# A second stopping place for GpSimd within each chunk's gathers, in the second sweep of a two-layer graph network

## The chip, the cores and the metric

The kernel runs on one core of one Trainium2 chip. The metric is the device time of one execution in microseconds; lower is better. The engines of the core are TensorE (PE, matmuls; PEld, its weight loads), VectorE (DVE), ScalarE (ACT), GpSimd (POOL) and SyncE (SP), which each work off a queue of their own and wait for one another through semaphores. GpSimd issues the indirect gathers here, SyncE nearly all the other transfers.

## The reference

Two layers over a graph of 12500 nodes with 128 features and 200000 edges (src, dst), the edges sorted by dst. A preceding layer norm and a relu stand before each layer, and each result is added to x.

```python
# layer 1
neigh = segment_sum(h[src], dst);  x = x + relu(relu(((1 + eps) * h + neigh) @ W1 + b1) @ W2 + b2)
# layer 2, on h = layernorm(relu(layernorm(x)))
t = gelu(concat([h[src], edge_vector], 1) @ Wt + bt)         # per edge
attn = sum((t @ Wk + bk) * (h[dst] @ Wq + bq), -1) * edge_type / sqrt(128)
e = exp(attn - segment_max(attn, dst)[dst]);  a = e / segment_sum(e, dst)[dst]
aggr = segment_sum(a * (t @ Wv + bv), dst);   x = x + (residual + gelu(aggr))
```

## The kernel before, in words

The 200000 edges are cut into 98 chunks of 2048 edges (CHUNK); a chunk is 16 columns of 128 edges, and four columns are a quad. The first sweep (`gin_sweeps`) does layer 1 and writes, for each node, its row of h @ Wt to DRAM (`source_rows`, `arow` in the code) and the vectors for the scores. The second sweep (`attention_sweeps`) does layer 2. It keeps running maxima and sums in windows of nodes, so that one pass over the chunks is enough.

In the second sweep, chunk c passes through stages; in step n each engine works on chunk n in the stage `f`, on n-1 as `mid`, on n-2 as `late`, on n-3 as `last` and on n-4 as `e`. The order within a step is written out by hand in the function `step` of each engine. The last four places of the pipeline matter less here; what counts is:

- GpSimd (lines 1115 to 1127) gathers the 16 columns of chunk c from `source_rows` into one of four buffers `t`, one indirect DMA per column (`gather_chunk`, issued in line 514), with a semaphore for each quad. It waits first for the chunk's list of sources, then for `t_used`, which counts the sums of chunk c-4 (the buffer's last reader), and then makes a `hold`: a multiplication of one element (line 508) that waits for the preceding hold's own count and so stands in GpSimd's queue as an instruction.
- TensorE, step n: turns quad 0 of chunk n into `pre_ps` and adds the edge features' product (lines 1140 and 1144), adds up the totals of n-3, turns quad 1, turns the gelu of quad 0 back (line 1153) and makes its score products (line 1167, semaphore `sc_q`, one count per quad), turns the scores of n-1, turns quad 2, then the gelu and the scores of quad 1, the block maxima of n-1 (line 1183), the end products of n-4, quads 3, 2 and 3 in the same manner, spreads the running maxima (line 1189), clears the sum banks and makes the sums of n-2 (line 1210, `t_used`, four counts per chunk).
- ScalarE makes the gelu of each quad (line 1281) and copies the turned result over the gathered rows in `t` (line 1285).
- VectorE adds the bias to the scores (line 1359), picks each edge's score, raises the window's maxima (line 1419) and keeps the accumulators.
- SP loads the list of sources, the edge features in two halves (line 1073), weights and windows. It loads the list of chunk c when the last quad of chunk c-2 has landed.

The first four steps and the last ones are written out, those between are a loop over four chunks each.

Of the kernel before, what the change touches and what calls it, by code (L numbers as in the profile page):

```python
# [43 lines left out]
QUADS = COLS // 4  # L44
# [31 lines left out]
def wait(eng, sem, value):  # L76

    if isinstance(value, int) and value <= 0:
        return
    eng.wait_ge(sem, value)  # L80
# [36 lines left out]
def over_chunks(eng, step):  # L117


    step(Chunk(None, 0), None)  # L120
    for n in range(1, PEEL):
        step(Chunk(None, n), Chunk(None, n - 1))
    with engine_loop(eng, 0, (NCH - PEEL - 2) // 4) as i:
        for n in range(PEEL, PEEL + 4):
            step(Chunk(i, n), Chunk(i, n - 1))
    for n in range(NCH - 2, NCH):
        step(Chunk(None, n), Chunk(None, n - 1))
    step(None, Chunk(None, NCH - 1))
# [375 lines left out]
def hold(gp, g, held, c):  # L504


    wait(gp, held, c)
    gp.tensor_tensor(g["spare"][0:1, 0:1], g["ones"][0:1, 0:1], g["ones"][0:1, 0:1], ALU.mult).then_inc(held, 1)  # L508


def gather_chunk(gp, idx, rows, out, done, op=ALU.bypass, cols=range(COLS)):

    for k in cols:
        gp.indirect_dma_start(out=out[:, k, :], out_offset=None, in_=rows[:, :], compute_op=op,  # L514
                              in_offset=bass.IndirectOffsetOnAxis(ap=idx[:, k:k + 1], axis=0)).then_inc(done, 16)
# [452 lines left out]
def attention_sweeps(nc, a, g, arow, qk, ck, fades, first, res, span):  # L968
# [4 lines left out]
    with ExitStack() as ctx:  # L973
# [37 lines left out]
        held = st.sem("held")  # L1011
# [9 lines left out]
        s = {k: st.sem("a_" + k) for k in names}  # L1021
# [34 lines left out]
        with nc.Fori(0, span + 1, WIN):  # L1056
            with nc.Block() as block:
# [57 lines left out]
                @block.gpsimd  # L1115
                def _(gp):
                    def step(f, bk):
                        if f:
                            if f.at == 3:
                                gp.wait_ge(w["tables"], 7)  # L1120
                            wait(gp, idx_in[f.j], 16 * (f.h + f.j))
                            wait(gp, s["t_used"], PARTS * (f.c - 3))
                            hold(gp, g, held, f.c)
                            for q in range(QUADS - 1 if f.last else QUADS):
                                gather_chunk(gp, g["idx0"] if f.at == 0 else idx[f.j], arow, t[f.k], gathered[f.k][q],
                                             cols=range(4 * q, 4 * q + 4))
                    over_chunks(gp, step)
# [395 lines left out]
```

## Time and profile before

| | us |
|---|---|
| median of 3 runs | 4087.96 (4086.41 to 4090.1) |
| span of the profiled execution | 6013.6 |
| POOL busy in it | 3043.9 |
| PE busy | 3985.3 |
| DVE busy | 1961.7 |
| ACT busy | 1601.6 |

The profiled execution is much longer than the timed ones. Its rows tell what each instruction took and what it waited for in that execution. An engine's idle time has a releaser: the work whose semaphore ended the wait; "issue" is idle time for which none is seen, and "remote" one whose source the profile doesn't tell. A time in a row of the timeline is the start since the beginning of the span.

### The profile page before, as it was taken

The page shows a single profiled execution, that of the slowest core. Times are in us where ns is not written, and L with a number is a line of the kernel's source. Part 1 is how long each engine was busy: PE and PEld are TensorE (multiplying, and loading weights), DVE is VectorE, ACT ScalarE, POOL GpSimd, SP SyncE. Part 2 cuts the span into 40 slices and gives each one's busy share as a digit, 9 for nine tenths or more (in the row PEclk, how much of TensorE's full clock was granted, in tenths as well). Part 3 has the DMA queues.
Part 4 walks back from the last instruction along what each step waited for, and adds up shares of the span by engine and source line. Part 5 has one row for each costly group of instructions (what it writes and reads, how often), then busy time and mean ns, then how long its engine had stood idle before and what let it go on. Part 6 is the DMA issues. An engine that isn't in the chain of part 4 may idle for free.

```text
span 6013.6 us, 75137 instructions
## 1 busy us (share of the span) xinstructions
PE 3985.3 (66%) x19120; PEld 3071.2 (51%) x19121; DVE 1961.7 (33%) x6898; ACT 1601.6 (27%) x3223; POOL 3043.9 (51%) x3332
## 2 busy tenths in 40 slices
PE   1466666555555555577777777777777777777777
PEld 1344444444434444355555555556555565555655
DVE  4222222222222222233333333333333333333344
ACT  4222222222222222322222222222222222222223
POOL 4566666666666666344444444444444444444442
PEclk5555555555565555577766667766676666766677
DMA  4122222222222222222222222222222222222222
GB/s 128 53 68 66 65 67 66 65 67 67 66 65 68 66 65 67 62 81 77 81 77 77 82 76 80 78 78 81 75 81 77 76 82 76 81 77 77 82 77 65
DMA packets 390065, 446.29 MB, mean 74 GB/s; under 512 B 111768, under 2 KB 314734, under 8 KB 390000
## 3 DMA queue, kind: packets, MB, share of 16 engines
q1 hardware_dynamic: 276940, 233.83, 13.3%
q0 software_dynamic: 100096, 205.20, 13.1%
q10 hardware_dynamic: 12964, 6.53, 0.4%
q8 instruction: 25, 0.41, 0.0%
q14 instruction: 40, 0.33, 0.0%
HBM read 387.05 MB, written 58.21 MB: 74 GB/s over the span
## 4 chain that ended last, share of the span: by engine, by line
another core or an unknown queue 28%; PE 25%; ACT 3%; issue 2%; DVE 0%; DVEq 0%; ACTq 0%
PE attention_sum_ps L1210 10%; PE attention_t_ps L1153 4%; PE attention_pre_ps L1144 3%; PE attention_sc_q L1167 3%; PE attention_row_bank L1189 2%; PE attention_pre_ps L1140 2%; ACT attention_tT L1281 2%; ACT attention_t L1285 1%; PE attention_tot_ps L1219 1%; PE attention_tot_ps L1202 1%; PE attention_sum_ps L1201 0%; DVE attention_lines L1419 0%; ACT acc L1043 0%; PE attention_xm_bank L1175 0%
## 5 line engine op out<-in xcount | busy, mean ns | idle before, releaser
L514 POOL DMA_INDIRECT attention_t<-source_rows,attention_idx x1548 | 1471.4, 951 | 496.0 <-issue 496.0
L514 POOL DMA_INDIRECT gin_hs<-h_rows,gin_idx x1500 | 1455.8, 971 | 486.1 <-issue 486.1
L508 POOL TENSOR_TENSOR spare<-ones 1x1 f32<-1x1 f32 x195 | 36.0, 184 | 1892.9 <-PE attention_sum_ps L1210 1376.9
L1281 ACT ACTIVATE attention_tT<-attention_pre_ps 128x512 f32<-128x512 f32 x391 | 233.5, 597 | 1883.5 <-remote 1381.9
L1167 PE MATMUL attention_sc_q<-attention_qw,attention_tT 128*128 x3128 | 590.7, 329 | 187.7 <-issue 187.6
L1167 PEld LDWEIGHTS attention_sc_q<-attention_qw,attention_tT 128*128 128x128 f32 x3128 | 540.7, 247 | 215.6 <-issue 215.4
L698 PE MATMUL gin_sums<-gin_hot,gin_hs 128*128 128x40 f32 x3136 | 612.2, 383 | 0.0
L1210 PE MATMUL attention_sum_ps<-attention_e_hot,attention_t 128*128 128x96 f32 x3072 | 607.5, 389 | 0.0
L698 PEld LDWEIGHTS gin_sums<-gin_hot,gin_hs 128*128 128x128 f32 x3136 | 598.1, 297 | 18.2 <-issue 12.6
L1210 PEld LDWEIGHTS attention_sum_ps<-attention_e_hot,attention_t 128*128 128x128 f32 x3072 | 591.8, 301 | 21.4 <-issue 20.9
L706 PE MATMUL gin_uy_bank<-acc,gin_w_W 128*128 x196 | 118.6, 708 | 727.2 <-DVE acc L926 727.1
L1419 DVE TENSOR_TENSOR attention_lines<-attention_lines,attention_row_bank 1x40 f32 x784 | 144.3, 184 | 1235.3 <-remote 1139.5
L1153 PE MATMUL attention_t_ps<-ident,attention_tT 128*128 128x128 f32 x1564 | 315.3, 338 | 340.4 <-ACT attention_t L1285 256.8
L1153 PEld LDWEIGHTS attention_t_ps<-ident,attention_tT 128*128 128x128 f32 x1564 | 229.1, 172 | 602.2 <-issue 314.8
L1144 PE MATMUL attention_pre_ps<-attention_evT,attention_w_edge 128*128 128x512 f32 x782 | 475.6, 695 | 0.0
L706 PEld LDWEIGHTS gin_uy_bank<-acc,gin_w_W 128*128 128x128 f32 x196 | 49.2, 312 | 763.9 <-issue 763.9
L1140 PE MATMUL attention_pre_ps<-ident,attention_t 128*128 128x128 f32 x1564 | 284.1, 311 | 208.5 <-issue 150.5
L926 DVE TENSOR_TENSOR acc<-acc,gin_sums 128x264 f32 x98 | 42.1, 430 | 1032.9 <-remote 1017.6
L1140 PEld LDWEIGHTS attention_pre_ps<-ident,attention_t 128*128 128x128 f32 x1564 | 199.5, 160 | 245.1 <-issue 179.8
L1285 ACT ACTIVATE attention_t<-attention_t_ps 128x512 f32<-128x512 f32 x391 | 232.9, 596 | 338.3 <-remote 253.5
L804 ACT ACTIVATE gin_n_zT<-gin_c_bank,eps 128x256 f32<-128x256 f32 x98 | 46.5, 474 | 980.1 <-remote 955.3
L1434 DVE TENSOR_TENSOR attention_masked<-attention_masked,attention_row_bank 128x80 f32<-128x80 f32 x784 | 126.6, 232 | 211.1 <-PE attention_row_bank L1189 210.8
(215 smaller groups left out, 5319.1 us busy)
## 6 DMA issues: line engine op xcount, KB each, us to landing
attention_evT<-in_edge_attr_cols SPq DMA_DIRECT2D x196, 512.0 KB
attention_t<-source_rows,attention_idx POOLq DMA_INDIRECT x1548
gin_hs<-h_rows,gin_idx POOLq DMA_INDIRECT x1500
attention_qw<-qk_cols SPq DMA_DIRECT2D x98, 160.0 KB, 3.2
attention_cw<-qk_bias_cols SPq DMA_DIRECT2D x98, 132.0 KB, 3.9
attention_fade<-fades SPq DMA_DIRECT2D x98, 132.0 KB, 3.8
gin_x<-in_x SPq DMA_DIRECT2D x98, 128.0 KB
residual_rows<-gin_r SPq DMA_DIRECT2D x98, 128.0 KB
```

Of the source, the lines that this page charges most:

```text
L514: gp.indirect_dma_start(out=out[:, k, :], out_offset=None, in_=rows[:, :], compute_op=op, in_offset=bass.IndirectOffsetOnAxis(ap=idx[:, k: ...
L698: mm = pe.matmul(sums[j][:, bass.ds(off, WIN)], hs[bk.k][:, k, :], hot[j][:, k, :], start=False, stop=True, skip_group_check=True)
L706: pe.matmul(u_ps, W["W1"][:, :], g["acc"][:, bass.ds(at, MW)], start=True, stop=False)
L1140: pe.matmul(pre_ps[:, k * P:(k + 1) * P], t[f.k][:, 4 * q + k, :], g["ident"][:, :], is_transpose=True, start=(k == 0), stop=False, skip_g ...
L1144: pe.matmul(pre_ps[:, :], w_edge[:, :], evT[q // 2][:, 512 * (q % 2):512 * (q % 2 + 1)], start=False, stop=True, skip_group_check=True).th ...
L1153: mm = pe.transpose(t_ps[:, k * P:(k + 1) * P], tT[q % 2][:, k * P:(k + 1) * P], g["ident"][:, :])
L1167: mm = pe.matmul(sc_ps[:, o:o + WIDE], tT[q % 2][:, (n % 4) * P:(n % 4 + 1) * P], qw[j][:, bass.ds(off, WIDE)], start=True, stop=True)
L1210: mm = pe.matmul(sum_of(bk)[:, bass.ds(off, WIDE)], t[bk.k][:, k, :], e_hot[j][:, k, :], start=False, stop=True, skip_group_check=True)
L1281: act.activation(tT[q % 2][:, :], pre_ps[:, :], ACT.Gelu).then_inc(s["tT_sb"], 1)
L1285: act.activation(t[f.k][:, 4 * q:4 * q + 4, :].rearrange("p k d -> p (k d)"), t_ps[:, :], ACT.Copy).then_inc(s["t_sb"], 1)
L1419: v.tensor_tensor(some, some, row_bank[0:1, b * WIN:(b + 1) * WIN], ALU.max).then_inc(s["raised"], 1)
L1434: v.tensor_tensor(masked[j][:, cols, :], masked[j][:, cols, :], row_bank[:, bass.ds(off, WIN)].unsqueeze(1).to_broadcast([P, SUB, WIN]), A ...
```

## The change

At half of a chunk's quads GpSimd waits until `sc_q` has reached 4(c-1) + 2, that is, until the score products of quads 0 and 1 of chunk c-1 are done, and makes a second hold. The hold's counter therefore goes up by two per chunk. The first sweep is as it was.

```diff
                             wait(gp, s["t_used"], PARTS * (f.c - 3))
-                            hold(gp, g, held, f.c)
+                            hold(gp, g, held, 2 * f.c)
                             for q in range(QUADS - 1 if f.last else QUADS):
+                                if q == QUADS // 2:
+                                    wait(gp, s["sc_q"], QUADS * (f.c - 1) + QUADS // 2)
+                                    hold(gp, g, held, 2 * f.c + 1)
                                 gather_chunk(gp, g["idx0"] if f.at == 0 else idx[f.j], arow, t[f.k], gathered[f.k][q],
                                              cols=range(4 * q, 4 * q + 4))
```

QUADS is 4 and PARTS is 4. For chunk 0 the value is negative and `wait` leaves the wait out.

## Rows read from the trace of the kernel before

**Rows 1.** The page: span, busy time, and the granted clock in 40 slices.
```profile
span 6013.6 us, 75137 instructions
...
PE 3985.3 (66%) x19120; PEld 3071.2 (51%) x19121; DVE 1961.7 (33%) x6898; ACT 1601.6 (27%) x3223; POOL 3043.9 (51%) x3332
...
PEclk5555555555565555577766667766676666766677
```

**Rows 2.** Groups on GpSimd, second sweep: busy us, mean ns, idle before, releasers.
```profile
L514 POOL DMA_INDIRECT attention_t<-source_rows,attention_idx x1548 | 1471.4, 951 | 496.0 <-issue 496.0
L508 POOL TENSOR_TENSOR spare<-ones 1x1 f32<-1x1 f32 x97 | 17.9, 184 | 1457.4 <-PE attention_sum_ps L1210 1376.9 <-issue 55.6 <-DMA attention_idx<-in_src_chunks 24.9
L514 POOL DMA_INDIRECT attention_t<-source_rows,idx x16 | 15.6, 975 | 5.1 <-issue 5.1
```

**Rows 3.** The same groups in the first sweep.
```profile
L514 POOL DMA_INDIRECT gin_hs<-h_rows,gin_idx x1500 | 1455.8, 971 | 486.1 <-issue 486.1
L514 POOL DMA_INDIRECT gin_hs<-in_x,gin_idx x44 | 42.7, 970 | 13.3 <-issue 13.3
L508 POOL TENSOR_TENSOR spare<-ones 1x1 f32<-1x1 f32 x97 | 17.9, 184 | 366.1 <-remote 257.0 <-DMA h_rows<-gin_hg 64.0 <-issue 29.2
```

**Rows 4.** Timeline, GpSimd, between the sweeps: start us, us, instruction, idle before.
```profile
2411.36 0.94 POOL L514 DMA_INDIRECT gin_hs<-h_rows,gin_idx  x1 [0.30 <-issue]
2481.72 0.18 POOL L508 TENSOR_TENSOR spare<-ones 1x1 f32<-1x1 f32 x1 [69.42 <-POOLq L234]
...
2501.65 0.94 POOL L514 DMA_INDIRECT attention_t<-source_rows,idx  x1 [0.30 <-issue]
2502.61 0.18 POOL L508 TENSOR_TENSOR spare<-ones 1x1 f32<-1x1 f32 x1
2502.94 0.98 POOL L514 DMA_INDIRECT attention_t<-source_rows,attention_idx  x1 [0.15 <-issue]
```

**Rows 5.** Timeline of a steady chunk: GpSimd, and one quad of TensorE.
```profile
4499.83 0.18 POOL L508 TENSOR_TENSOR spare<-ones 1x1 f32<-1x1 f32 x1 [15.57 <-PE attention_sum_ps L1210]
...
4500.49 0.98 POOL L514 DMA_INDIRECT attention_t<-source_rows,attention_idx  x1 [0.48 <-issue]
...
4504.74 0.60 PE L1140 MATMUL attention_pre_ps<-ident,attention_t 128*128 128x128 f32 x4
...
4506.48 1.03 PE L1167 MATMUL attention_sc_q<-attention_qw,attention_tT 128*128 x8
...
4509.28 0.95 POOL L514 DMA_INDIRECT attention_t<-source_rows,attention_idx  x1 [0.30 <-issue]
...
4519.29 0.95 POOL L514 DMA_INDIRECT attention_t<-source_rows,attention_idx  x1 [0.30 <-issue]
...
4535.04 0.18 POOL L508 TENSOR_TENSOR spare<-ones 1x1 f32<-1x1 f32 x1 [14.81 <-PE attention_sum_ps L1210]
...
4535.71 0.98 POOL L514 DMA_INDIRECT attention_t<-source_rows,attention_idx  x1 [0.48 <-issue]
```

**Rows 6.** Timeline of the same chunk: ScalarE and VectorE, released by TensorE.
```profile
4520.97 0.60 ACT L1285 ACTIVATE attention_t<-attention_t_ps 128x512 f32<-128x512 f32 x1 [4.30 <-remote]
...
4523.35 2.39 DVE L1419 TENSOR_TENSOR attention_lines<-attention_lines,attention_row_bank 1x40 f32 x8 [11.89 <-remote]
```

**Rows 7.** Timeline, TensorE: the sums and the first half of the next step.
```profile
4529.03 5.85 PE L1210 MATMUL attention_sum_ps<-attention_e_hot,attention_t 128*128 128x96 f32 x32
...
4534.72 0.60 PE L1140 MATMUL attention_pre_ps<-ident,attention_t 128*128 128x128 f32 x4
...
4541.69 0.47 PE L1167 MATMUL attention_sc_q<-attention_qw,attention_tT 128*128 x3
```

**Rows 8.** Timeline, GpSimd: the last gather of the execution.
```profile
5944.36 0.94 POOL L514 DMA_INDIRECT attention_t<-source_rows,attention_idx  x1 [0.30 <-issue]
```

**Rows 9.** All holds: duration in ns, shortest, median, longest.
```profile
L508 POOL TENSOR_TENSOR spare<-ones x195: 184/184/188, 34.0 to 5929.9; 1x1 f32<-1x1 f32 x195
```

**Rows 10.** Groups between 4000 and 5000 us: two of VectorE's with two SBUF inputs.
```profile
L1389 DVE TENSOR_TENSOR acc<-acc,attention_fade 128x264 f32 x28 | 12.0, 428 | 2.9 <-issue 2.9
...
L1422 DVE TENSOR_TENSOR attention_mdiff<-rows,attention_lines 1x264 f32<-1x264 f32 x28 | 11.8, 422 | 1.0
```

## The prediction

> **What bounds the kernel now.** I read the head of the page first, because its span and the time to be predicted differ: the profiled execution spans 6013.6 us [rows 1], the median of the unprofiled runs is 4088.0 us, with a spread of 4 us. The recorded execution is 1.47 times as long as the ones that are timed. So no row may be taken over as a share of the time; what is to be asked of each row is whether it can still be true when 1925 us are gone. No time of the profiled execution other than its span is given, so the sum below is made in steps of the span and carried to the median by a budget.
>
> The second view is GpSimd alone, once for each sweep. In the second sweep it issued 1548 + 16 indirect gathers of 951 ns and 975 ns with 496.0 + 5.1 us of idle time between them that nothing released ("issue", some 0.3 us each), and 97 one-element multiplications (the holds) of 17.9 us in all: 1471.4 + 15.6 + 496.0 + 5.1 + 17.9 = 2006.0 us of work. Beside it stand 1457.4 us of idle time ahead of the holds, nearly all released by the sums on TensorE [rows 2]. In the first sweep the same sum is 1455.8 + 42.7 + 486.1 + 13.3 + 17.9 = 2015.8 us, with 366.1 us of waiting [rows 3]. Both sweeps need 4022 us of GpSimd, and some 60 us less if no hold has to be woken (below). The whole unprofiled execution takes 4088. The 1457 + 366 us of waiting at the holds must therefore be almost entirely an effect of the recorded execution: in the timed runs GpSimd works from end to end. What is left is 66 to about 126 us. The start takes 34.0 of them up to the first hold [rows 9], and the gap between the sweeps (2412.3 to 2481.7, 69.4 us here [rows 4]) and the end after the last gather (5945.3 to 6013.6, 68.3 us here [rows 1, 8]) want more than the remaining 32 to 92 us already.
>
> The third view is TensorE in a steady chunk. Its first half, from the turning of quad 0 to the scores of quad 1, goes from 4534.72 to 4541.69 + 1.03 = 4542.7 us at the full clock: 8.0 us [rows 7], the last 1.03 being what eight score products take at 4506.48 [rows 5]. The rest I estimate from rows of the same clock: two quads of 4504.74 to 4507.51 = 2.8 us [rows 5] less some 1.3 us for the turning of quad 2, which is counted already, the sums with 5.85 us [rows 7], and 2.5 to 3.7 us, a guess, for spreading the maxima, the end products and the clearing. That gives about 20.6 to 21.8 us per chunk as recorded, against 2006.0 / 98 = 20.5 us for GpSimd. The two engines are level in the second sweep, within what these rows can tell; the budget above says that TensorE can't be much over 20.7 us either. I take it that the bound of the second sweep is GpSimd or a tie, and that the granted clock is near full there: the trace has 6 and 7 tenths [rows 1], but with TensorE waiting a large part of its step.
>
> **The change, part by part.** Three things change, all on GpSimd's queue in the second sweep.
>
> First, the hold at a chunk's start waits for the count 2c instead of c. It is the hold's own counter and it is already there. No cost.
>
> Second, each of the 98 chunks gets a second hold after its second quad of gathers. What a hold costs when nothing keeps it waiting is seen at the second chunk: the last gather of chunk 0 starts at 2501.65, the hold at 2502.61, the first gather of chunk 1 at 2502.94 [rows 4]. From gather to gather that is 1.29 us. Without a hold it is (4509.28 - 4500.49) / 7 = 1.256 us [rows 5]. So an unhindered hold costs 0.04 us, since it slips into the 0.3 us between gathers: 98 x 0.04 = 4 us if GpSimd sets the end, 0 if TensorE does. When it does have to wait, waking costs more: from the hold's start to the next gather 4535.71 - 4535.04 = 0.67 us [rows 5] against 0.33 us unhindered, so 0.38 us in all beyond the wait, or 98 x 0.38 = 37 us. No unhindered hold stands inside the loop in this trace, where the wait's value is also computed in registers; for that the 0.38 us is the upper end too. I take 0.04, since that row is the same instruction in the same place of the queue, already satisfied.
>
> Third, the wait itself. Behind it on GpSimd's queue are the eight gathers of quads 2 and 3 of chunk c, then everything of chunk c+1; the list loads are SP's and are not queued behind it, but SP waits for the last quad of a chunk before it overwrites its list, so it inherits a delay. It is released by the score products of quad 1 of chunk c-1. The earliest start of chunk c's gathers is the end of the sums of chunk c-4, which is the start of TensorE's step c-1. The eight gathers and the hold then need 4509.28 + 0.95 - 4499.83 = 10.4 us [rows 5]; TensorE needs 8.0 us from the start of that step [rows 7]. So even where GpSimd is as far ahead as it may be, the release comes 2.4 us before it is asked for, and where GpSimd is behind (it is the bound) it comes earlier still. Wait: 0.
>
> A cover that is gone must be priced too. Suppose the release comes x us into the step, later than 10.4. Quads 2 and 3 then end at x + 0.7 + 10.0, so the next chunk starts x + 10.7 - P into the next step of length P, and its own first half ends 10.4 us after that, which is past x whenever 21.1 > P. The wait does not add up from chunk to chunk: it moves idle time from the chunk's start to its middle. TensorE feels it only if quad 3 is late for its turning, about 9 us into step c: for P = 20.6 with some 2 us for a landing, x would have to exceed 16 us.
>
> A hold could also be held up by VectorE, if the two meet at SBUF. A step has five VectorE instructions with two SBUF inputs (fades and maxima), 0.42 us each [rows 10], 2.1 us of 20.6; a tenth of the new holds would meet one and wait some 0.2 us: 98 x 0.1 x 0.2 = 2 us more. Against it, all 195 holds of the trace lie between 184 and 188 ns [rows 9], though VectorE was busy for a third of the span [rows 1]. This is rival (d). The Trainium skill, in "SBUF — State Buffer", section "Who interferes with whom", has the rule behind it: a VectorE instruction with two SBUF inputs contends with a GpSimd instruction that reads SBUF, and the later one blocks. The trace does not bear it out for the holds.
>
> Sum: 4088 + 4 us if GpSimd bounds the second sweep, 4088 + 0 if TensorE does. I forecast 4091 us.
>
> **The rivals.** (a) The wait bites, and the time ends above. The recorded execution speaks for it. There TensorE's completions reach the others late: ScalarE copies quad 1 only at 4520.97 us, and VectorE starts raising the maxima, released by a product queued right behind the scores of quad 1, at 4523.35 us [rows 6]. The step began at about 4499.8, so x is between 21 and 23.5 us of 35.2. The same share of a step of 20.6 us would be 12 to 14 us, past 10.4. Then GpSimd wakes at each middle, 0.38 us, and where it is the bound that is 98 x 0.38 = 37 us: 4125 us. It decides from the point at which the scores of quad 1 come more than 10.4 us after the gathers' start while GpSimd has no idle time elsewhere. Against it: a wait delays the next chunk, and from then on the release is earlier than the demand, so not every chunk would pay. A milder form, 0.1 to 0.2 us per hold for the registers in the loop, gives 4098 to 4108 us. Chance 0.25 for both.
>
> (b) The pause helps TensorE. In the trace its completions stay away just while gathers are issued (4500.5 to 4520.2) and come in a rush afterwards [rows 5, 6]. If a rest of that exists without the recording, a pause at a chunk's middle lets them through. Against it: GpSimd is busy for nearly the whole timed execution, so a pause that is really taken costs what it gives. The most that can be won is what GpSimd idles in the second sweep; of the 32 to 92 us left in the budget, which the gap and the end want as well, I let a third of the upper figure lie there: 4088 - 30 = 4058 us. Chance 0.18.
>
> (c) The change does nothing to time because the second sweep is bound by TensorE, whose steps GpSimd's holds cannot reach: 4088 us. This and the +4 us of the forecast can't be told apart here; both are "no change". Together 0.52.
>
> (d) VectorE's two-input instructions hold up some of the new holds. With one in ten late by 0.2 us it is 4088 + 4 + 2 = 4094 us. The even durations of all holds [rows 9] speak against it. Chance 0.05.
>
> **How the numbers follow.** About 0.2%, 8 us, is what a measurement of this kernel tells from no change. Forecast, (c) and (d), 4088 to 4096: 0.52 + 0.05 = 0.57, same. Rival (a), 4098 to 4125: 0.25, slower. Rival (b), 4058 to 4079: 0.18, faster. The range takes in both ends of the hold's cost and both rivals' prices: 4058 to 4126 us.
>
> **What the changed profile would show.** The holds would be 293 instead of 195, with 184 ns each. In the second sweep a middle hold would follow the eighth gather. In the recorded execution, where completions are late, I expect it to wait: from about 10.4 to some 23 us into the chunk, 11 to 13 us each. The last eight gathers then end near 33.9 us, just before the release of the next chunk at 35.2 us [rows 5], so the idle time ahead of the first hold shrinks from about 15 to 1 to 3 us and the span stays near 6010 us. If the span of the second sweep falls instead, completions were held back by the gathers, and (b) gains. If it grows by more than 1%, the wait bites and (a) gains. The prediction is wrong in its root if an unhindered hold in the loop is seen to cost more than 0.1 us from gather to gather, or if the gathers themselves are faster without the recording, so that GpSimd isn't the bound at all and TensorE's waits decide.

## The result and the profile after

| | us |
|---|---|
| before, median of 20 runs | 4088.1 (4080.8 to 4094.4) |
| after, median of 20 runs | 4095.7 (4086.8 to 4106.9) |
| ratio | 1.002, 95% interval 1.0013 to 1.0027 |
| forecast | 4091, range 4058 to 4126 |
| span of the profiled execution, before / after | 6013.6 / 4085.1 |

The change costs 7.6 us, 0.2%. The forecast said +3 and named no measurable change as the likeliest; the time lies in the range and just within the border, 4096 us, of what it called the same. The range is 68 us wide, so that the time fell into it says little; the terms are what is to be compared.

The profiled execution of the changed kernel is as long as the timed ones. Its page:

```profile
span 4085.1 us, 75424 instructions
...
PE 3302.9 (81%) x19120; PEld 2576.1 (63%) x19121; DVE 1932.0 (47%) x6898; ACT 1590.1 (39%) x3223; POOL 3046.0 (75%) x3430
...
PEclk6555555565655565555679999999999999999999
```

So much shorter a recording looks like a large gain of the change. It is none: the kernel before, recorded again, has a span of 4094.3 us (below). The 6013.6 us of [rows 1] belonged to that one recording. What produced it stays open; no run here tries it.

GpSimd in the second sweep, first after the change, then in the new recording of the kernel before; columns as in [rows 2], which they answer:

```profile
L514 POOL DMA_INDIRECT attention_t<-source_rows,attention_idx x1548 | 1481.2, 957 | 442.2 <-issue 428.1 <-PE attention_sc_q L1170 5.3 <-DMA attention_idx<-in_src_chunks 4.6
L508 POOL TENSOR_TENSOR spare<-ones 1x1 f32<-1x1 f32 x196 | 36.6, 187 | 31.4 <-POOLq L234 28.1
L514 POOL DMA_INDIRECT attention_t<-source_rows,idx x16 | 15.8, 990 | 4.9 <-issue 4.8 <-POOL spare L508 0.2
```

```profile
L514 POOL DMA_INDIRECT attention_t<-source_rows,attention_idx x1548 | 1479.6, 956 | 456.9 <-issue 452.5 <-DMA attention_idx<-in_src_chunks 4.0
L508 POOL TENSOR_TENSOR spare<-ones 1x1 f32<-1x1 f32 x98 | 18.4, 188 | 34.3 <-POOLq L234 32.5
L514 POOL DMA_INDIRECT attention_t<-source_rows,idx x16 | 15.6, 974 | 5.1 <-issue 5.1
```

The 1457.4 us of waiting ahead of the holds [rows 2] are gone in both: what is left is the gap between the sweeps, at the first hold. Without that gap, GpSimd works through the second sweep in 1481.2 + 442.2 + 36.6 + 15.8 + 4.9 = 1980.7 us after and 1479.6 + 456.9 + 18.4 + 15.6 + 5.1 = 1975.6 us before. Nor does any of the 98 new holds wait; the 5.3 us put down to `attention_sc_q` are 19 ordinary gaps of 0.3 us ahead of gathers. The groups leave out idle times as short as the 0.02 us ahead of a hold, so the length of the sweep tells more. From the start of its first gather to the end of its last one it took 1983.3 us after and 1976.7 us before: 6.6 us more, 0.07 us per new hold.

That the new recording of the kernel before is nevertheless the longer of the two, by 9.2 us, comes mostly from the first sweep, whose code is the same. From its first hold to its last gather it took 2001.1 us before and 1989.5 us after. One recording of each kernel can't show a change of 0.2%; why the first sweep varies is found below.

The timeline around a chunk's start (the hold at 3007.37) and its middle (3017.63) after the change, start and duration in us:

```profile
3005.74 1.03 PE L1170 MATMUL attention_sc_q<-attention_qw,attention_tT 128*128 x8
...
3006.41 0.94 POOL L514 DMA_INDIRECT attention_t<-source_rows,attention_idx  x1 [0.30 <-issue]
...
3007.37 0.18 POOL L508 TENSOR_TENSOR spare<-ones 1x1 f32<-1x1 f32 x1
...
3007.71 0.98 POOL L514 DMA_INDIRECT attention_t<-source_rows,attention_idx  x1 [0.15 <-issue]
...
3008.99 0.94 POOL L514 DMA_INDIRECT attention_t<-source_rows,attention_idx  x1 [0.30 <-issue]
...
3009.09 0.65 PE L1143 MATMUL attention_pre_ps<-ident,attention_t 128*128 128x128 f32 x4 [0.54 <-DMA attention_t<-source_rows,attention_idx]
...
3014.28 3.81 PE L1213 MATMUL attention_sum_ps<-attention_e_hot,attention_t 128*128 128x96 f32 x32
...
3017.63 0.18 POOL L508 TENSOR_TENSOR spare<-ones 1x1 f32<-1x1 f32 x1
```

Two things are to be read in it. TensorE waits for GpSimd, at quad 3 (3009.09), whose last gather has just landed; it follows GpSimd and not the other way round. It made the scores of quad 1 by 3006.8 us; the middle hold of the next chunk asks for them at 3017.6, 10.9 us later. And the price of a hold is complete only at the second gather behind it: from 3006.41 to 3008.99 are 2.58 us for two gathers, where two without a hold take 2.50. The hold fits into the idle 0.30 us all but some 0.05, and the gather behind it takes 0.98 us instead of 0.94.

### The profile page after: what moved, and what is told of

It reads as the page before. It is cut to its first block and busy times, and to the rows that moved or that the text cites. A ratio compares the mean times of both kernels' runs of the same rounds, so it can differ in the third digit from the quotient of the medians.

```text
span 4085.1 us, 75424 instructions
## 1 busy us (share of the span) xinstructions
PE 3302.9 (81%) x19120; PEld 2576.1 (63%) x19121; DVE 1932.0 (47%) x6898; ACT 1590.1 (39%) x3223; POOL 3046.0 (75%) x3430
## 5 line engine op out<-in xcount | busy, mean ns | idle before, releaser
L514 POOL DMA_INDIRECT attention_t<-source_rows,attention_idx x1548 | 1481.2, 957 | 442.2 <-issue 428.1
L514 POOL DMA_INDIRECT gin_hs<-h_rows,gin_idx x1500 | 1428.1, 952 | 443.8 <-issue 443.4
L698 PE MATMUL gin_sums<-gin_hot,gin_hs 128*128 128x40 f32 x3136 | 683.1, 412 | 0.0
L698 PEld LDWEIGHTS gin_sums<-gin_hot,gin_hs 128*128 128x128 f32 x3136 | 668.7, 328 | 22.3 <-issue 21.6
L1147 PE MATMUL attention_pre_ps<-attention_evT,attention_w_edge 128*128 128x512 f32 x782 | 420.6, 621 | 1.7 <-issue 1.7
L1170 PE MATMUL attention_sc_q<-attention_qw,attention_tT 128*128 x3128 | 409.8, 275 | 0.0
L1170 PEld LDWEIGHTS attention_sc_q<-attention_qw,attention_tT 128*128 128x128 f32 x3128 | 388.4, 195 | 0.0
L692 PE MATMUL gin_sums<-gin_zeros 1*128 1x264 bf16 x98 | 36.2, 369 | 412.5 <-DMA gin_hs<-h_rows,gin_idx 264.0
L1213 PE MATMUL attention_sum_ps<-attention_e_hot,attention_t 128*128 128x96 f32 x3072 | 365.9, 277 | 0.0
L1213 PEld LDWEIGHTS attention_sum_ps<-attention_e_hot,attention_t 128*128 128x128 f32 x3072 | 350.2, 192 | 11.9
L1156 PE MATMUL attention_t_ps<-ident,attention_tT 128*128 128x128 f32 x1564 | 245.6, 281 | 0.0
L492 ACT ACTIVATE gin_m_std<-gin_m_mv,ln_eps 128x2 f32<-128x2 f32 x294 | 85.2, 290 | 340.0 <-DVE gin_m_mv L486 339.5
```

The costliest lines, as they stand in the source:

```text
L492: act.activation(m["std"][:, :], m["mv"][:, :, 1], ACT.Sqrt, bias=g["ln_eps"][:, 0:1]).then_inc(s["std"], 1)
L698: mm = pe.matmul(sums[j][:, bass.ds(off, WIN)], hs[bk.k][:, k, :], hot[j][:, k, :], start=False, stop=True, skip_group_check=True)
L1147: pe.matmul(pre_ps[:, :], w_edge[:, :], evT[q // 2][:, 512 * (q % 2):512 * (q % 2 + 1)], start=False, stop=True, skip_group_check=True).th ...
L1156: mm = pe.transpose(t_ps[:, k * P:(k + 1) * P], tT[q % 2][:, k * P:(k + 1) * P], g["ident"][:, :])
L1170: mm = pe.matmul(sc_ps[:, o:o + WIDE], tT[q % 2][:, (n % 4) * P:(n % 4 + 1) * P], qw[j][:, bass.ds(off, WIDE)], start=True, stop=True)
L1213: mm = pe.matmul(sum_of(bk)[:, bass.ds(off, WIDE)], t[bk.k][:, k, :], e_hot[j][:, k, :], start=False, stop=True, skip_group_check=True)
```

## Experiments

**The kernel before once more.**

> The unchanged kernel once more, for a second profiled execution of it and as a measure of what two equal kernels show against each other. Ratio 1.000 within 0.001 by every theory. If the 6013.6 us span of the first profiled execution was an effect of that one recording, the span is now near 4088 us, all holds of the second sweep are unwaited, and its 98 chunks take some 1975 us from first to last gather. If the change itself took the stalls away that the first profile showed, the span is again near 6000 us.

Ratio 0.9996 (0.9987 to 1.0005), span 4094.3 us. The long recording isn't the kernel's. That also removes the only support for the rival in which the pause helps TensorE: the 1457.4 us of waiting in which the late completions showed [rows 2] aren't there.

**The hold without the wait.**

```diff
                                 if q == QUADS // 2:
-                                    wait(gp, s["sc_q"], QUADS * (f.c - 1) + QUADS // 2)
                                     hold(gp, g, held, 2 * f.c + 1)
```

> The second hold in each chunk of the second sweep without the wait for the score products. In the profile after the change all 195 holds of the second sweep are unwaited; between the gathers around one lie 0.356 us instead of 0.305, and the gather behind it takes 0.983 us instead of 0.945. Theory 1, the hold's own place in the queue costs 0.05 + 0.04 = 0.09 us and the wait nothing: +8.7 us, 1.0021, the same as the whole change. Theory 2, the wait or the coupling to TensorE costs: no more than 4 us, under 1.001.

1.0022 (1.0013 to 1.0031), against 1.002 (1.0013 to 1.0027) of the whole change. The wait adds nothing that these runs can tell, which is some 5 us by the two intervals; the hold is the change's cost.

**Three more holds per chunk.**

```diff
-                                if q == QUADS // 2:
-                                    wait(gp, s["sc_q"], QUADS * (f.c - 1) + QUADS // 2)
-                                    hold(gp, g, held, 2 * f.c + 1)
+                                if q > 0:
+                                    hold(gp, g, held, QUADS * f.c + q)
```

> Holds ahead of quads 1, 2 and 3 of each chunk of the second sweep (three more than before, not one), with no wait for the scores. Theory 1, 0.09 us per hold: 3 x 98 x 0.089 = +26 us, 1.0064. If a hold costs 0.04 us as predicted: +12 us, 1.003. If the loss came from the wait: 1.000.

1.0059 (1.0045 to 1.0074), or some 24 us for 293 holds: 0.08 us each, 0.06 to 0.10 by the interval. In the recording the second sweep is 2004.4 us long, 27.7 more than before or 0.09 per hold. That is the first theory's figure and excludes both others.

**One more hold per chunk in the first sweep instead.**

```diff
-                            hold(gp, g, held, f.c - 1)
+                            hold(gp, g, held, 2 * (f.c - 1))
...
-                                             cols=range(AHEAD if f.at == 1 else 0, COLS))
+                                             cols=range(AHEAD if f.at == 1 else 0, COLS // 2))
+                                hold(gp, g, held, 2 * f.c - 1)
+                                gather_chunk(gp, idx[f.k], rows, hs[f.k], gathered[f.k], cols=range(COLS // 2, COLS))
```

> One more hold in the middle of each full chunk's gathers in the first sweep (97 of them), none in the second, no wait. Theory 1, every hold costs GpSimd 0.09 us wherever GpSimd is the bound: +8.6 us, 1.0021, as in the second sweep. If the loss needs the second sweep's coupling to TensorE: 1.000.

1.0052 (1.0038 to 1.0066): 21 us, neither of the two. The gathers of the first sweep had become longer. First the trace of this kernel, then the new one of the kernel before:

```profile
L514 POOL DMA_INDIRECT gin_hs<-h_rows,gin_idx x1500 | 1457.6, 972 | 429.5 <-issue 418.7 <-POOL spare L508 10.8
```

```profile
L514 POOL DMA_INDIRECT gin_hs<-h_rows,gin_idx x1500 | 1440.3, 960 | 443.7 <-issue 443.4 <-DMA gin_idx<-in_src_chunks 0.3
```

17.3 us of busy time more; 97 x 0.04 = 4 us of it is the known surplus of the gather behind a hold. The rest are single gathers of up to 1.6 us. What stands beside one shows in the timeline of the kernel before:

```profile
1157.94 0.82 DVE L440 TENSOR_TENSOR gin_hot<-iota,rel 128x640 f32<-128x640 f32 x1
1158.00 1.58 POOL L514 DMA_INDIRECT gin_hs<-h_rows,gin_idx  x1 [0.30 <-issue]
...
1159.88 0.94 POOL L514 DMA_INDIRECT gin_hs<-h_rows,gin_idx  x1 [0.30 <-issue]
```

VectorE's comparison of two SBUF operands runs from 1157.94 to 1158.76; the gather that begins within it takes 0.64 us more. The count of 34 long gathers in the expectation below goes with all 98 comparisons, of which nearly every one overlaps some gather; what matters is the start. In the kernel before, 46 of the gathers of `h_rows` start while such a comparison runs, and 31 of these take more than 1.0 us. With the extra hold, which moves the gathers against VectorE, it is 49 of 58. The long ones start 0.04 us or more after the comparison did, and end 0.81 to 0.86 us after its end, as if begun only then. Over the six recordings whose first sweep has the same code (before again, after, `hold_only`, `three_holds`, `later_release`, `own_scores`) the count of such long gathers goes from 13 to 31 and the busy time of the group from 1428.1 to 1440.3 us, so how often the two meet varies from execution to execution. A new theory: such a comparison and the start of a gather get in each other's way at SBUF.

**The comparison with one operand in PSUM.** Free columns of the bank that the chunk's sums will use hold the row of numbers; TensorE doesn't write this bank before the comparison is done.

```diff
+        for j in range(2):
+            nc.vector.tensor_copy(sums[j][:, SPAN:SPAN + WIN], g["iota"][:, :]).then_inc(spot_ready, 1)
-        nc.vector.wait_ge(spot_ready, 2)
+        nc.vector.wait_ge(spot_ready, 4)
...
-                            onehot_op(v, g, hot[f.j], f.c, g["iota"][:, :]).then_inc(hot_ready, 1)
+                            onehot_op(v, g, hot[f.j], f.c, sums[f.j][:, SPAN:SPAN + WIN]).then_inc(hot_ready, 1)
```

> No second hold. In the first sweep the comparison that makes the one-hot (line 440) reads the row of numbers from PSUM instead of SBUF, so that it has one SBUF input instead of two; all else as before. In the second profile of the kernel before, 34 of the 98 such instructions that overlapped the start of a gather went with a gather of over 1.0 us, up to 1.58 instead of 0.94. If the two meet at SBUF: these gathers shrink, up to 34 x 0.6 = 20 us less, 0.995 to 0.998. If the long gathers have another cause: 1.000.

0.9973 (0.9964 to 0.9983). The gathers of the first sweep, as above:

```profile
L514 POOL DMA_INDIRECT gin_hs<-h_rows,gin_idx x1500 | 1420.7, 947 | 443.8 <-issue 443.2 <-DMA gin_idx<-in_src_chunks 0.3 <-PE gin_sums L700 0.3
```

They take 19.6 us less than in the kernel before, whose recording is the highest of the six; against the lowest it is 7.4 us. The timed runs of this comparison differ by 12.9 us in the median. The comparison itself is no faster, 0.82 us, and a gather that starts within it isn't longer:

```profile
353.10 0.82 DVE L440 TENSOR_TENSOR gin_hot<-gin_sums,rel 128x640 f32<-128x640 f32 x1
353.22 0.94 POOL L514 DMA_INDIRECT gin_hs<-h_rows,gin_idx  x1 [0.30 <-issue]
```

Of the 32 gathers of `h_rows` that start during a comparison here, none takes more than 0.98 us. The kernel before has the same control within its own trace: in the second sweep the comparison of the same shape reads `attention_tot_ps`, which is in PSUM, and of the 71 gathers that start during it none takes more than 0.98 us.

**Both.** The PSUM row and the extra hold of the first sweep.

> The same, with one more hold in the middle of each chunk of the first sweep. Without the PSUM row that hold cost 21 us instead of 9; in its trace 51 of the 98 comparisons fell on the start of a gather that was then long, instead of 34. If the surplus of 12 us came from this meeting, it goes away: this kernel is slower than the one with the PSUM row alone by 9 us (0.002) and no more, so 0.997 to 1.000 of the kernel before. If the surplus has another cause: 0.005 above the one with the PSUM row alone.

0.9997 (0.9988 to 1.0007), which is 0.0024 or 10 us above the one with the PSUM row alone. The hold again costs 0.1 us, and the surplus of 12 us is gone with the two-operand comparison: of 60 gathers that start during a comparison none is long. The new theory holds.

**A later release, and one that bites.** The change with another value of the wait:

```diff
-                                    wait(gp, s["sc_q"], QUADS * (f.c - 1) + QUADS // 2)
+                                    wait(gp, s["sc_q"], QUADS * f.c)
```

> The change with its wait moved from the score products of the first two quads to those of all four quads of the preceding chunk. In the profile after the change the middle hold at 3017.63 us comes 10.9 us after the end of the scores of quad 1 (3006.8) and 4.3 us after those of quad 3 (3013.4). Theory 1 (a wait that is over before it is asked for costs nothing, only the hold's place does): all holds of the second sweep stay unwaited and it is +8 us, 1.002, as with the change. If the coupling costs by itself: more than with the change, over 1.004.

1.0032 (1.0022 to 1.0042): between the 1.002 of the first theory and the 1.004 from which the other would have begun, and the interval overlaps that of the change. Three holds waited, 1.0 us together. Whether a later release costs the few microseconds by which this median lies above that of the change (11.2 against 7.6 us) isn't shown. Then the scores of the chunk's own quad 0 (the value `QUADS * f.c + 1`):

> The change with its wait moved on to the scores of quad 0 of the chunk's own gathers, which TensorE can only make after quad 1 has landed. That is the pause that bites: from the middle hold's place (3017.6 us in the profile after the change) to the end of those scores (3022.9) are 5.3 us, and 0.3 us more for waking. As GpSimd is the bound, 98 x 5.6 = +550 us, 1.13. If GpSimd had slack to give in the second sweep, as the rival with TensorE helped by a pause needs: much less, under +150 us.

1.1712 (1.1684 to 1.1739), 699 us more. All holds of the execution, and what they waited for:

```profile
L508 POOL TENSOR_TENSOR spare<-ones x293: 184/184/213, 34.1 to 4739.9; 1x1 f32<-1x1 f32 x147
...
  PE attention_sc_q L1170: 657.8, 98
```

The pause is 657.8 / 98 = 6.7 us per chunk, not the 5.3 I had read off: TensorE is further behind at the middle of the chunk. At the chunk around 3500 us its sums end 1.8 us after the hold's turn, where they ended 0.5 us after it in the trace of the change. With 0.3 us for waking that is 98 x 7.0 = 690 us. Every microsecond in which GpSimd really stops comes out in the time. It has no idle time to give.

**Fewer holds.** With the PSUM row, one hold for two chunks in the loop of the first sweep, waiting for what both need:

```diff
-                            wait(gp, idx_in[f.k], listed(f))
-                            wait(gp, sums_ready, f.c - 3)
-                            hold(gp, g, held, f.c - 1)
+                            if f.at is None or f.at > 7:
+                                if f.n % 2 == 0:
+                                    ahead = Chunk(f.base, f.n + 1)
+                                    wait(gp, idx_in[f.k], listed(f))
+                                    wait(gp, idx_in[ahead.k], listed(ahead))
+                                    wait(gp, sums_ready, ahead.c - 3)
+                                    hold(gp, g, held, f.h + 3)
```

(before chunk 8 as it was)

> The row of numbers in PSUM, as in iota_psum, and in the loop of the first sweep a hold for every second chunk only, which waits for what both chunks need. 45 holds fewer. If an unhindered hold costs 0.09 us in both directions: 4 us less than iota_psum alone, so 0.9963 of the kernel before instead of 0.9973. If the wait for the second chunk's buffer, asked for one chunk earlier, is not over by then: slower than iota_psum, and waits appear ahead of the holds of the first sweep.

0.9999 (0.999 to 1.0008): a miss. The waits on GpSimd, engine and releaser, with total, times and longest in us, name it:

```profile
POOL spare L508 <- PE gin_sums L708: 26.3, 1, 26.3
```

It is the first paired hold. In the start of the sweep TensorE is still behind, and asking for its sums one chunk early waits 26.3 us where the single hold of the kernel with the PSUM row waits 9.8. That is 16.5 us more, less the 4 that the missing holds give back; the measured loss is 0.0026, 11 us. No later hold of the sweep waits. So the pairs were made to begin at chunk 12:

> As iota_psum_paired, but the pairs begin at chunk 12 instead of chunk 8. In the trace of iota_psum_paired the first paired hold waited 26.3 us at 229.7 us for the sums, where the single one of iota_psum waited 9.8; all later ones waited for nothing. If that one wait was the loss: gone, and with 43 holds fewer 4 us less than iota_psum, 0.996 to 0.997 of the kernel before. If holds for two chunks cost something all along: again near 1.000.

> iota_psum once more, on the same chip as the kernel with late pairs: 0.997 of the kernel before, by both theories.

0.9936 (0.9923 to 0.995) with the late pairs and 0.9951 (0.9938 to 0.9965) without pairs, on one chip: medians 4075.9 and 4083.4, 7.5 us for 43 holds where 4 were expected. The intervals overlap; the direction is that of the theory, and the loss of the early pairs is gone. In the two recordings the first sweep is, from first hold to last gather, 1980.6 and 1984.8 us long, 4.2 us apart, which is the 4 expected; the rest lies elsewhere and isn't explained by the holds. The kernel with the PSUM row alone stands at 0.9973 on one chip and 0.9951 on another, so ratios from different chips are not to be compared to 0.001. This kernel beats both the one before and the changed one.

## Why the prediction was right, and where it wasn't

**The bound** was named rightly, and by the budget rather than by the rows: 4022 us of GpSimd work can't be in 4088 us beside 1800 us of waiting. The 4022 us were too many, since they hold the waking at each hold and the longer gathers of the long recording: in the new recording the two sweeps need 1975.6 us and 1440.3 + 443.7 + 43.5 + 13.3 + 18 = 1959 us, together 3934. The conclusion stands: no hold of the second sweep waits, and TensorE waits for the gathers. The pause of 6.7 us that cost 7.1 proves it.

**The tie with TensorE** was wrong. I put a step of TensorE at 20.6 to 21.8 us, with the sums at 5.85 us as if at full clock [rows 7]. The first half of the next step, from 4534.70 to 4542.80, was indeed at a granted clock of 1.00, the full 2.4 GHz, but that of the sums was 0.61, a mix of 1.2 and 2.4 GHz:

```profile
4529.00:4534.60 5.60, 5.60 (x32) 5.58 (x32) 4.97 (x20) 3.65 (x6) 0.00 (x0) 0.61 0.10 25
```

(From and to, the length, busy time and instructions of PE, PEld, DVE, ACT and POOL, granted clock, DMA share, GB/s.) After the change the sums take 3.81 us at a granted clock of 1.00 (3014.28), 2 us less. With that the estimate is 18.6 to 19.8 us, below the 1976.7 / 98 = 20.2 us of GpSimd. So forecast (c), no cost because TensorE bounds, falls.

**The cost of an unhindered hold** is the term that was mis-sized: 0.04 us predicted, 0.08 measured (7.6 us for 98 holds, 24 us for 293; 0.1 in the first sweep without the long gathers). The row that I used was the right one and I stopped one gather too early. I measured from the gather ahead of the hold to the start of the gather behind it, 1.29 us. That the gather behind it then takes 0.98 us instead of 0.94 to 0.95 stood in the same rows, [rows 4, 5]. With it the sum is 98 x 0.08 = 8 us and the forecast 4096. The forecast of +3 lay near the 7.6 measured because both of its errors, the half price and the half-believed tie, are small beside 4088 us.

**The wait** cost nothing, as predicted, and for the stated reason, though the margin is larger: 10.9 us instead of 2.4, since GpSimd is 8.5 us behind its earliest start.

**Rival (a)** with its 37 us for waking didn't occur; its milder form, 0.1 us per hold for the registers in the loop, gives nearly the measured time by a cause that the rows don't bear out. In the loop the next gather starts 1.30 us after the one ahead of the hold (3006.41 to 3007.71), in the written-out step it is 1.29 us [rows 4]; what the sum lacked lies in the length of the gather behind. **Rival (b)** had its whole support in the long recording. **Rival (d)**, VectorE's two-operand instructions, I gave 0.05 because all 195 holds took 184 to 188 ns [rows 9]. That evenness belonged to that recording too. In the new recording of the kernel before the longest takes 833 ns, and after the change 509 ns:

```profile
L508 POOL TENSOR_TENSOR spare<-ones x293: 182/183/509, 34.2 to 4030.8; 1x1 f32<-1x1 f32 x147
```

Their sum is small, 54.9 us for 293 at 187 ns in the mean, so the term stays near nothing for the holds. But I looked for it at the holds alone. The gathers, whose list of sources lies in SBUF, meet VectorE as well, and there it is worth 0.3 to 0.5% of this kernel.

**The profile after** was predicted from the disturbed recording (middle holds waiting 11 to 13 us, a span near 6010) and isn't like that in any point but the number of the holds, 293, and their usual length, 183 ns.

## What to carry to other kernels

Where one engine works from end to end, an instruction added to its queue can cost more than it moves the next one's start, since that one may itself become longer; read two instructions far. When the span of a profiled execution and the timed runs differ by half, make a budget of busy time against the timed runs before any wait is believed. And a pause put into the bound engine was, in these runs, either free because it never happened, or cost its full length.

## What the runs showed of the hardware

An indirect gather on GpSimd that begins while VectorE runs an instruction with two SBUF operands takes up to 0.65 us longer, 1.60 instead of 0.94 us. The long ones end 0.81 to 0.86 us after the end of that instruction. Of the 32 gathers of `h_rows` that started more than 0.035 us into a 128x640 comparison of the kernel before, 31 took more than 1.0 us. It is not longer beside the same instruction with one operand in PSUM: none of 32 with the row of numbers moved, none of 71 in the second sweep of the kernel before. In the timed runs this was worth 0.0027 of the time on one chip and 0.0049 on another. The Trainium skill, in "SBUF — State Buffer", section "Who interferes with whom", states the contention for GpSimd instructions that read SBUF. For a `tensor_tensor` of VectorE it infers there that descriptor generation isn't stalled, since this takes the write side; by these runs, an indirect gather is held up. Which part of the gather it is that waits was not tried.

A gather behind a one-element multiplication on GpSimd takes 0.98 us, behind another gather 0.94. Why was not tried.
